# Weight sums on TensorE, a split soft-max in a new order, and a fourth pair of PSUM banks for one tile

## The chip, the cores and the metric

The kernel runs on one core of a Trainium2 chip. The metric is the device time of one execution in microseconds; the median of several runs is compared. Engines: PE is TensorE, DVE is VectorE, ACT is ScalarE, POOL is GpSimd, SP is SyncE (it only issues DMAs here).

## The reference

`x` is 8 images of 64 channels, 48 x 48 pixels, 32-bit. The reference normalises it by groups of two channels, makes from the result 8 logits a pixel (a 1x1 convolution) and a soft-max over them, makes 8 convolutions 3x3 (64 to 64 channels each), and adds, pixel by pixel, their weighted sum to `x`.

```python
def _gn(v, G=32, eps=1e-05): ...        # (v - mean) / sqrt(var + eps) over 2 channels x 48 x 48
...
logits = conv(x, coupler_w) + coupler_b[None, :, None, None]    # 8 sets
sel = softmax(logits, axis=1)
sel = sel / sel.sum(axis=1, keepdims=True)
conv = conv3x3(x, w).reshape(b_, s, oc, h_, w_) + bias[None, None, :, None, None]
return einsum('bschw,bshw->bchw', conv, sel)
...
x = x + _L0_conv_ref(_gn(x), ...)
```

## The kernel before, in words

**Work.** Two images at a time (a round; 4 rounds), their 128 channels on the 128 partitions. The 3x3 convolution uses a short form along the row: two neighbouring pixels are made of four products ("points") in place of six. For each point the input is a sum or difference of columns (`v_pts`) and the weights are sums of the three kernel columns: point 1 is w0 + w2 + w1, point 2 is w0 + w2 - w1 (both halved), the last two are w0 and w2. A round has 18 tiles (`TILES`) of 128 pixel pairs. Every factor is split in a 16-bit head and a 16-bit tail, so that a point is 4 or 5 matmuls of 512 columns (8 sets x 64 channels): three heads (one for each kernel row `r`) and one or two with tails (`point`). A tile has a pair of PSUM banks. PE writes points 1 and 2 into it (`first_points`); ACT copies bank 0 (`copy_m1`); DVE makes sum and difference (`seed`), which are the two pixels; PE adds points 3 and 4 (`last_points`); DVE multiplies by the selection (`multiply`, two passes), adds halves (`halve`), and POOL does the rest (`finish`).

**Banks.** Three pairs, `pair[i % 3]`, and two single banks: `side` with the logits and group sums, `w_bank` with the bound of the weights and warming matmuls.

**The start.** Each engine has a queue written out by hand, and the order of the calls at the end of its block is the order of execution. SP loads image pair 0 in three parts, two small matrices (for the group mean) and the weights `w_raw` in three rows, 768 KB each; then `first_fill(g, part)` copies input points from `v_head` and `v_tail` to the matmul operands `op` and `op_two`, five DMAs a call. ACT takes the largest absolute weight (`bound_of`), DVE and PE make of it one scale for all (`weight_bound`, L459 and L460, `scales`). DVE makes the sums of weights: `kernel_sum(r)` is w0 + w2 (L930), `kernel_point1(r)` adds w1 (L935), `kernel_point2()` subtracts it, all rows in one pass (L941). ACT rounds these to heads (`w_heads_of`, L607), DVE makes the tails (`first_point_tails` L917, `second_point_tails` L924, `last_point_tails` L948 and L951). The input has the same: heads on ACT (`first_heads`, L527), tails on DVE (`input_tails_of`, L977), for the first 24 image rows (part 0) and the rest (part 1). POOL makes the raw input points 1 to 3 (L1083), but its last two wait for the first weight head (`w_heads[0]`).

**Soft-max.** For the first round it is in two parts: the first 12 of 36 pixel columns before tile 0, the rest in pieces after tiles 0 to 3. `with_bias` is L713, `maximum` L720, `selection` L765 and L766. DVE's first pass of tile 0 (`multiply`, L791) waits for the first selection. After tile 4 `combine` makes the moments of the next image pair.

**PE's order at the start**: warming matmuls, group sums, warming matmuls of 32-bit ones (L450), the two bound matmuls, ten wide warming matmuls (L464), point 1 of tiles 0 and 1, the logits (54 small matmuls, L380), point 2 of tiles 0 and 1, both of tile 2, then the round: after the last points of tile i come the first points of tile i + 2. `load_ahead(1)` (ACT) loads the next image pair when all input points are made.

## Time and profile before

| | |
|---|---|
| median of 3 runs | 346.08 us (345.93 to 346.24) |
| profiled execution: time, span | 345.96 us, 344.2 us |
| mean granted clock of PE | 0.986 |
| PE busy | 325.8 us, 95% of the span |
| DVE busy | 282.4 us, 82% |
| POOL busy | 229.9 us, 67% |
| PE weight loads, beside the matmuls | 157.3 us, 46% |
| ACT busy | 108.9 us, 32% |

The span is from the first to the last instruction of the one execution that was profiled. A share is over the whole span and says nothing of a stage. A row of the timeline gives start and duration in us, engine, line, operation, output and inputs, shape and count; the next instruction of an engine may start before the one ahead has ended, so the cost of one is the distance of two starts.

### The profile page before, as it was taken

Reading aid. Unit: us, or ns where it says so; the run is one execution under the profiler, and the core shown is the slowest. Engines: PE = TensorE matmul, PEld = TensorE weight load, DVE = VectorE, ACT = ScalarE, POOL = GpSimd, SP = SyncE. Lnnn points to the kernel's source line nnn. Section 1 sums busy time; section 2 is a strip of 40 time slices with the busy share of each in tenths; the row PEclk is TensorE's granted clock in tenths of the full one; section 3 lists DMA queues with packets and bytes.
Section 4 is the critical chain, followed back from the end, with each engine's and each line's share of the span. In section 5 each row is a group of like instructions: output and inputs, shape, how many; then the busy total and the mean of one; then the engine's idle time right before and its main releaser. Section 6 shows DMA issues by size and latency. Waiting matters only on the chain.

```text
span 344.2 us, 5508 instructions
## 1 busy us (share of the span) xinstructions
PE 325.8 (95%) x1730; PEld 157.3 (46%) x1730; DVE 282.4 (82%) x508; ACT 108.9 (32%) x159; POOL 229.9 (67%) x329
## 2 busy tenths in 40 slices
PE   8959599999999899999999999999999899999993
PEld 8924244444544344444544344444544344444441
DVE  2789999997799697877799688887799687777786
ACT  1758262155411152164411152164411111111110
POOL 3420288899995489899874489899863499433343
PEclk9987999999999999999999999999999999999998
DMA  6543989507980298008980297009830496001002
GB/s 215 218 89 82 268 211 213 126 0 195 215 222 2 73 239 182 1 0 212 186 235 1 81 231 179 0 0 234 178 80 0 112 237 146 0 24 46 1 1 69
DMA packets 30230, 41.34 MB, mean 120 GB/s; under 512 B 2112, under 2 KB 23232, under 8 KB 29824
## 3 DMA queue, kind: packets, MB, share of 16 engines
q1 hardware_dynamic: 29328, 37.49, 45.9%
q10 hardware_dynamic: 880, 3.58, 3.4%
q8 instruction: 10, 0.16, 0.2%
q14 instruction: 12, 0.10, 0.1%
HBM read 11.97 MB, written 4.72 MB: 48 GB/s over the span
## 4 chain that ended last, share of the span: by engine, by line
PE 72%; DVE 23%; issue 4%; DVEq 1%; POOL 0%; POOLq 0%
PE pair L390 41%; PE pair L402 14%; PE pair L398 10%; PE w_bank L450 5%; DVE high L792 4%; DVE pair L791 3%; DVE half L800 3%; DVE pair L777 2%; DVE pair L775 2%; PE side L380 1%; DVE v_tail L977 1%; DVE w_tail L948 1%; DVE w_tail L917 1%; DVE w_tail L924 1%; DVE mix L759 0%
## 5 line engine op out<-in xcount | busy, mean ns | idle before, releaser
L390 PE MATMUL pair<-w_head,op 128*128 128x512 f16 x864 | 234.7, 381 | 9.0 <-DVE half L800 4.9
L390 PEld LDWEIGHTS pair<-w_head,op 128*128 128x128 f16 x864 | 83.4, 98 | 113.0 <-DVE half L800 9.5
L402 PE MATMUL pair<-w_tail,op 128*128 128x512 f16 x288 | 109.7, 381 | 0.5 <-DVE w_tail L951 0.5
L577 ACT ACTIVATE m_sb<-pair 128x512 f32<-128x512 f32 x72 | 42.9, 596 | 202.4 <-PE pair L402 194.0
L1106 POOL TENSOR_TENSOR quarter<-half 128x256 f32<-128x256 f32 x71 | 52.7, 742 | 64.6 <-DVE half L800 63.9
L791 DVE TENSOR_TENSOR pair<-pair,sel_now 128x512 f32<-128x512 f32 x71 | 49.4, 696 | 39.0 <-PE pair L402 38.9
L800 DVE TENSOR_TENSOR half<-pair,high 128x512 f32<-128x512 f32 x71 | 49.1, 692 | 9.5
L398 PE MATMUL pair<-w_tail,op_two 128*128 128x512 f16 x144 | 54.6, 379 | 0.1
L775 DVE TENSOR_TENSOR pair<-pair,m_sb 128x512 f32<-128x512 f32 x72 | 49.6, 689 | 0.0
L777 DVE TENSOR_TENSOR pair<-m_sb,pair 128x512 f32<-128x512 f32 x72 | 49.3, 684 | 0.0
L792 DVE TENSOR_TENSOR high<-pair,sel_now 128x512 f32<-128x512 f32 x71 | 48.3, 680 | 0.0
L402 PEld LDWEIGHTS pair<-w_tail,op 128*128 128x128 f16 x288 | 28.3, 98 | 34.9 <-DVE w_tail L951 0.8
L1110 POOL TENSOR_TENSOR mixed<-quarter 128x128 f32<-128x128 f32 x71 | 32.8, 462 | 5.6
L1116 POOL TENSOR_TENSOR y_out<-mixed,x_res 128x128 f32<-128x128 f32 x71 | 32.4, 457 | 5.7 <-POOL mixed L1110 0.3
L1069 POOL TENSOR_TENSOR v_tail<-v_pts,v_head 128x576 f16<-128x576 f32 x24 | 30.4, 1289 | 0.0
L398 PE MATMUL pair<-w_tail,op 128*128 128x512 f16 x72 | 27.8, 386 | 1.4 <-DVE w_tail L917 1.4
L1099 POOL TENSOR_TENSOR x_res<-x_res,bias_part 128x384 f32<-128x384 f32 x24 | 24.1, 1004 | 3.1 <-DMA x_res<-x_pix 0.6
L1078 POOL TENSOR_TENSOR v_pts<-x_raw 128x1152 f32<-128x1152 f32 (+1 forms) x12 | 24.9, 2078 | 0.0
L398 PEld LDWEIGHTS pair<-w_tail,op_two 128*128 128x128 f16 x144 | 14.1, 98 | 17.5 <-DVE w_tail L948 0.6
L1094 POOL TENSOR_TENSOR bias_part<-bias_all,sel_now 128x384 f32<-128x384 f32 x24 | 19.9, 829 | 0.1
L450 PE MATMUL w_bank<-ones 128*128 128x128 f32 x116 | 16.0, 308 | 1.6 <-POOL v_tail L1138 1.6
L450 PEld LDWEIGHTS w_bank<-ones 128*128 128x128 f32 x116 | 15.7, 223 | 1.6 <-POOL v_tail L1138 1.6
(107 smaller groups left out, 192.3 us busy)
## 6 DMA issues: line engine op xcount, KB each, us to landing
op<-v_head SPq DMA_DIRECT2D x14, 600.0 KB, 8.2
x_res<-x_pix SPq DMA_DIRECT2D x8, 576.0 KB, 6.5
op_two<-v_head SPq DMA_DIRECT2D x14, 300.0 KB, 9.2
op<-v_tail SPq DMA_DIRECT2D x14, 300.0 KB, 6.2
op<-v_head SPq DMA_DIRECT2D x14, 288.0 KB, 8.5
out<-y_out SPq DMA_DIRECT2D x7, 576.0 KB, 3.9
x_raw<-x ACTq DMA_DIRECT2D x3, 1152.0 KB, 9.7
w_raw<-weight SPq DMA_DIRECT2D x3, 768.0 KB, 8.5
```

What stands on the lines that cost most here:

```text
L390: nc.tensor.matmul(dst, op[b][:, 0, j, at + r * PW:at + r * PW + P], w_head[:, j, r, :], start=fresh and r == 0, stop=False, skip_group_ch ...
L398: nc.tensor.matmul(dst, op[b][:, 0, j, after] if j == 0 else op_two[b][:, j - 2, after], w_tail[:, j, 1, :], start=False, stop=False, skip ...
L402: return nc.tensor.matmul(dst, op[b][:, 1, j, at:at + P], w_tail[:, j, 0, :], start=False, stop=True, skip_group_check=True)
L450: nc.tensor.matmul(w_bank[:, 2 * P:3 * P], ones[:, :], ones[:, :], start=True, stop=True)
L577: act.activation(m1_sb[:, i % LOOK, :], pair[i % SETS_OF_BANKS][:, 0, :], ACT.Copy).then_inc(m1_copied, 1)
L775: dve.tensor_tensor(plus, minus, m1, ALU.add).then_inc(seeded, 1)
L777: dve.tensor_tensor(minus, m1, minus, ALU.subtract).then_inc(seeded, 1)
L791: dve.tensor_tensor(sets_of(i, 0), sets_of(i, 0), weights_of(i, 0), ALU.mult).then_inc(low_done, 1)
L792: dve.tensor_tensor(high[:, :, :, :], sets_of(i, SETS // 2), weights_of(i, SETS // 2), ALU.mult) \
L800: dve.tensor_tensor(half[:, i % LOOK, :, :, :].rearrange("p a s c -> p a (s c)"), pair[i % SETS_OF_BANKS][:, :, 0:N // 2], high[:, :, :, : ...
L1106: pool.tensor_tensor(quarter[:, :, :, :].rearrange("p a s c -> p a (s c)"), hf[:, :, 0:2, :].rearrange("p a s c -> p a (s c)"), hf[:, :, 2 ...
L1110: pool.tensor_tensor(mixed[:, :, :], quarter[:, :, 0, :], quarter[:, :, 1, :], ALU.add).then_inc(mixed_done, 1)
```

## The change

- `kernel_sum`, `kernel_point1` and `kernel_point2` of DVE go. PE makes point 1 of the weights: for each row three 32-bit matmuls of 512 columns with an identity matrix (a third matrix in `mats`) add w0, w2, w1 in PSUM, in banks of `pair[2]` and `pair[1]`. ACT and DVE read it there. DVE makes point 2 as point 1 - 2 w1, one pass a row.
- PE's 30 warming matmuls of 32-bit ones after the group sums go, and the ten wide ones become six. The bound matmuls come after seven of the nine new ones.
- The head of input point 0, part 0, is made by DVE (`first_head`). DVE's order changes: the input tails of all points of part 0 come before those of part 1 and before the tails of point 2 of the weights. ACT's order changes too; its edges come earlier.
- POOL's wait for `w_heads[0]` goes.
- Two of the five DMAs of the first fill are issued by ACT; the residual load `load_res(0, 0)` comes after the first fill and not after the third; `load_ahead(1)` comes after the heads of point 1 of the weights.
- `side` and `w_bank` become a fourth pair, `spare`, which tile 3 of the first round uses. PE makes point 1 of tiles 0, 1, 2, then point 2 of the same, the logits, then both of tile 3. In the first round tile i + 3 is begun after the last points of tile i, for i from 1 to 3. From tile 4 on the pair is `pair[(i + 2) % 3]`.
- The bias pass of the soft-max is one over all 36 pixel columns (the logits must leave `side` before tile 3 fills it); the pieces of the second part come partly one tile later, its last ones after tile 4.

```diff
-WARM_SMALL = (28, 30)
-WARM_WIDE = 10
+WARM_SMALL = 28
+WARM_WIDE = 6
-BIAS_FIRST_AT = (0, 0, 3, 4, 10, 13)
+BIAS_FIRST_AT = (0, 0, 4, 4, 10, 13)
...
-        side = ctx.enter_context(nc.psum_tensor("side", [P, N], F32))
-        w_bank = ctx.enter_context(nc.psum_tensor("w_bank", [P, N], F32))
+        spare = ctx.enter_context(nc.psum_tensor("spare", [P, 2, N], F32))
+        w_bank, side = (spare[:, a, :] for a in range(2))
+        w_pt1 = [pair[2][:, 0, :], pair[2][:, 1, :], pair[1][:, 1, :]]
...
+        def banks_of(i, begin=False):
+            if begin and i <= SETS_OF_BANKS:
+                return (pair + [spare])[i]
+            return pair[(i + SETS_OF_BANKS - 1) % SETS_OF_BANKS]
... SP
             first_fill(0, 0)
+            load_res(0, 0)
             first_fill(1, 0)
             first_fill(0, 1)
-            load_res(0, 0)
             first_fill(1, 1)
... PE, first_point
+                if not begin or i >= 2 * SETS_OF_BANKS + 1:
+                    pe.wait_ge(half_done, n * TILES + i + 1)
+                elif i > SETS_OF_BANKS:
+                    pe.wait_ge(half_done, i)
+                elif i == SETS_OF_BANKS and a == 1:
+                    pe.wait_ge(prep, 7)
... PE, start
-            warm_small(WARM_SMALL[1])
+            def kernel_point1(r, columns):
+                for kx in columns:
+                    last = nc.tensor.matmul(w_pt1[r], eye_mat[:, :], w_raw[:, r, kx, :], start=kx == 0, stop=kx == 1)
+                return last
+            pe.wait_ge(w_loaded[0], 16)
+            kernel_point1(0, (0, 2, 1)).then_inc(w_point1, 1)
+            pe.wait_ge(w_loaded[1], 16)
+            kernel_point1(1, (0, 2, 1)).then_inc(w_point1, 1)
+            pe.wait_ge(w_loaded[2], 16)
+            kernel_point1(2, (0,))
             (the two bound matmuls)
+            kernel_point1(2, (2, 1)).then_inc(w_point1, 1)
...
-            for i in range(2):
-                first_point(i, 0, 0, i == 0)
+            for i in range(3):
+                first_point(i, 0, 0, i == 0, True)
+            for i in range(3):
+                first_point(i, 1, 0, i == 0, True)
             (logits)
-            for i in range(2):
-                first_point(i, 1, 0, i == 0)
-            first_points(2, 0)
+            first_points(3, 0, True)
... ACT, the weight heads and the start
+                if k == 0 and rows.start < 2:
+                    act.wait_ge(w_point2, rows.stop)
...
+            def fill_beside():
+                pts, cols = slice(0, 2), slice(0, PW + FIRST_PAIRS)
+                act.wait_ge(h_first, 2)
+                act.dma_start(op[0][0:C, 1, pts, cols], v_head[0:C, pts, cols]).then_inc(first_in[0], 16)
+                act.dma_start(op_two[0][C:P, :, cols], ...).then_inc(first_in[0], 16)
             bound_of(2)
-            first_heads(0, 0)
+            fill_beside()
+            act.wait_ge(scale_ready, 1)
+            for k in range(2, NP):
+                edge(0, k)
+            first_heads(2, 0)
             act.wait_ge(w_chain, W_STEPS)
             (the three heads of point 1)
+            load_ahead(1)
+            first_heads(3, 0)
+            w_heads_of(1)
             first_heads(1, 1)
             first_heads(0, 1)
-            first_heads(2, 0)
-            w_heads_of(1)
-            first_heads(3, 0)
             w_heads_of(2)
             copy_m1(0, 0)
             w_heads_of(3)
... DVE, after the weight bound
-            kernel_sum(0) ... kernel_point1(2) ... kernel_point2()
+            def kernel_point2(r):
+                dve.wait_ge(w_point1, r + 1)
+                if r == 2:
+                    dve.wait_ge(w_heads[0], K)
+                dve.scalar_tensor_tensor(w_pt2[:, r, :], w_raw[:, r, 1, :], -2.0, w_pt1[r], ALU.mult, ALU.add) \
+                    .then_inc(w_point2, 1)
...
             first_input_point(0)
             input_tails_of(1, 0, 1)
+            first_head()
+            input_tails_of(0, 0, 2)
             first_input_point(1)
             weight_bound()
+            kernel_point2(0)
             scales()
+            kernel_point2(1)
+            first_point_tail(0)
+            first_point_tail(1)
+            kernel_point2(2)
+            first_point_tail(2)
+            input_tails_of(2, 0, 3)
+            input_tails_of(3, 0, 4)
+            second_point_tails()
             coupler_parts()
             input_tails_of(1, 1, 1)
             input_tails_of(0, 1, 2)
+            last_point_tails(2, 0)
+            last_point_tails(2, 1)
+            with_bias(0)
+            seed(0, 0, begin=True)
             maximum(0, 0)
             less_maximum(0, 0)
+            last_point_tails(3, 0)
             add_up(0, 0)
... POOL
-            pool.wait_ge(w_heads[0], 1)
```

The lines in brackets stand for lines that are unchanged.

## Rows read from the trace of the kernel before

**Rows 1.** Busy time by stages: stretch, its length, busy us (instructions) of each engine

```profile
core 0: us, PE busy (x) PEld busy (x) DVE busy (x) ACT busy (x) POOL busy (x), PEclk, DMA share, GB/s
10.00:20.00 10.00, 9.63 (x80) 8.73 (x80) 7.15 (x21) 6.89 (x10) 2.41 (x5) 1.00 0.44 155
20.00:30.00 10.00, 6.61 (x70) 2.97 (x69) 9.83 (x15) 6.73 (x10) 2.33 (x2) 0.70 0.23 49
...
150.00:250.00 100.00, 99.19 (x557) 46.40 (x556) 81.00 (x141) 38.41 (x53) 80.24 (x105) 1.00 0.57 133
```

**Rows 2.** Waits from 60 us to the end: total us, times, longest

```profile
PE pair L390 <- DVE half L800: 3.5, 4, 1.7
```

**Rows 3.** Timeline of DVE, the weights and the first input points

```profile
12.68 0.82 DVE L972 SCALAR_TENSOR_TENSOR v_pts<-x_raw,twice_mean 128x576 f32<-128x576 f32 x1
...
13.42 0.81 DVE L977 SCALAR_TENSOR_TENSOR v_tail<-v_pts,norm_scale,v_head 128x576 f16<-128x576 f32 x1
14.15 0.68 DVE L930 TENSOR_TENSOR w_sum<-w_raw 128x512 f32<-128x512 f32 x1
...
14.86 0.69 DVE L935 TENSOR_TENSOR w_pts<-w_sum,w_raw 128x512 f32<-128x512 f32 x1
...
15.47 0.82 DVE L972 SCALAR_TENSOR_TENSOR v_pts<-x_raw,twice_mean 128x576 f32<-128x576 f32 x1
...
17.53 0.14 DVE L984 TENSOR_REDUCE w_max<-w_max_part 64x1 f32<-64x3 f32 x1
...
18.43 0.16 DVE L989 TENSOR_SCALAR magnitude<-w_bank 128x2 int32<-128x2 int32 x1 [0.76 <-PE w_bank L460]
...
19.77 0.69 DVE L930 TENSOR_TENSOR w_sum<-w_raw 128x512 f32<-128x512 f32 x1
...
20.49 1.18 DVE L935 TENSOR_TENSOR w_pts<-w_sum,w_raw 128x512 f32<-128x512 f32 x1
21.60 0.77 DVE L959 TENSOR_SCALAR cw_pts<-cw_pair,half_scale 128x32 f16<-128x32 f32 x1
...
25.08 1.75 DVE L941 TENSOR_TENSOR w_pts<-w_sum,w_raw 128x1536 f32<-128x1536 f32 x1
```

**Rows 4.** Timeline of DVE, the soft-max and the first tiles

```profile
31.90 0.31 DVE L713 SCALAR_TENSOR_TENSOR logit<-side,undo,cb_all 128x96 f32<-128x96 f32 x1
...
41.05 0.70 DVE L791 TENSOR_TENSOR pair<-pair,sel_now 128x512 f32<-128x512 f32 x1
...
43.08 0.41 DVE L713 SCALAR_TENSOR_TENSOR logit<-side,undo,cb_all 128x192 f32<-128x192 f32 x1
...
61.37 0.69 DVE L775 TENSOR_TENSOR pair<-pair,m_sb 128x512 f32<-128x512 f32 x1
```

**Rows 5.** POOL's last input points in the timeline, and all passes of L700 (ns min/median/max)

```profile
19.97 2.37 POOL L1083 TENSOR_TENSOR v_pts<-x_raw 128x368 f32<-128x368 f32 x2 [7.59 <-ACT w_head L607]
...
L700 DVE SCALAR_TENSOR_TENSOR shift<-group,norm_scale x3: 271/274/1295, 71.7 to 225.7; 128x1 f32<-128x1 f32 x3
```

**Rows 6.** Timeline of PE: 32-bit warming matmuls, and two starts of a tile

```profile
10.85 6.94 PE L450 MATMUL w_bank<-ones 128*128 128x128 f32 x60
...
43.22 0.82 PE L390 MATMUL pair<-w_head,op 128*128 128x512 f16 x3 [1.46 <-DVE half L800]
...
47.33 0.81 PE L390 MATMUL pair<-w_head,op 128*128 128x512 f16 x3
```

**Rows 7.** Timeline, all engines: first weight heads, the fifth DMA, the first point

```profile
16.41 0.76 ACT L527 ACTIVATE v_head<-v_pts,norm_scale 128x576 f16<-128x576 f32 x1
...
19.17 1.33 ACT L607 ACTIVATE w_head<-w_pts,half_scale 128x512 f16<-128x512 f32 x2 [2.00 <-DVE scale L996]
...
20.01 0.59 SPq L308 DMA_DIRECT2D op<-v_tail  x1
...
23.02 0.82 PE L390 MATMUL pair<-w_head,op 128*128 128x512 f16 x3 [1.97 <-DMA op<-v_tail]
```

**Rows 8.** Two stretches of 1 us: PE's busy time, granted clock, DMA share, GB/s

```profile
24.00:25.00 1.00, 0.00 (x0) 0.52 0.00 0
...
30.00:31.00 1.00, 1.00 (x5) 0.56 0.08 20
```

More of the change, by code:

```diff
@@ L113, in program @@
         bias_all = sb("bias_all", [P, C])
[L114 to L115 removed]
+        mats = sb("mats", [P, 3, P])
+        mean_mat, diff_mat, eye_mat = (mats[:, k, :] for k in range(3))
         minus_half = sb("minus_half", [P, 1])
@@ L299, in first_fill @@
                 sp.dma_start(op[0][0:C, 0, pts, cols], heads[:, :, cols]).then_inc(landed, 16)
-                sp.dma_start(op[0][0:C, 1, pts, cols], heads[:, :, cols]).then_inc(fifth, 16)
+                if g or part:
+                    sp.dma_start(op[0][0:C, 1, pts, cols], heads[:, :, cols]).then_inc(fifth, 16)
                 sp.dma_start(op[0][C:P, 1, pts, below], heads[:, :, above]).then_inc(landed, 16)
-                if g == 0:
+                if g == 0 and part == 0:
+                    pass
+                elif g == 0:
                     sp.dma_start(op_two[0][C:P, :, cols], v_head[0:C, 1, cols].unsqueeze(1).to_broadcast([C, 2, width])) \
@@ L429, in last_points @@
                     pe.wait_ge(seeded, n * 2 * TILES + 2 * i + a + 1 + 2 * LOOK)
-                    point(b, 2 + a, t, pair[s][:, a, :], False, begin and i == 0).then_inc(y_done, 1)
+                    point(b, 2 + a, t, banks_of(i, begin)[:, a, :], False, begin and i == 0).then_inc(y_done, 1)
             def round_(n, more, begin=False):
@@ L522, in first_heads @@
                 act.wait_ge(v_first[k], ((1, 2), (2, 3), (2, 3), (2, 3))[k][part])
-                if k >= 2 and part == 0:
-                    edge(0, k)
+                if k >= 2:
                     act.wait_ge(edge_done, k - 1)
@@ L576, in copy_m1 @@
                 act.wait_ge(seeded, n * 2 * TILES + 2 * i + 2)
-                act.activation(m1_sb[:, i % LOOK, :], pair[i % SETS_OF_BANKS][:, 0, :], ACT.Copy).then_inc(m1_copied, 1)
+                act.activation(m1_sb[:, i % LOOK, :], banks_of(i, n == 0)[:, 0, :], ACT.Copy).then_inc(m1_copied, 1)
             def round_(n, more, ahead, copied=0):
@@ L766, in selection, with seed @@
                 dve.tensor_scalar(dst[0][:, px, :], mix[:, px, :], undo[:, 0:1], None, ALU.mult).then_inc(done, 1)
-            def seed(i, n, pixels=(0, 1)):
-                plus, minus = (pair[i % SETS_OF_BANKS][:, a, :] for a in range(2))
+            def seed(i, n, pixels=(0, 1), begin=False):
+                plus, minus = (banks_of(i, begin)[:, a, :] for a in range(2))
                 m1 = m1_sb[:, i % LOOK, :]
```

135 lines of the change are left out of this document (57 added, 78 removed).

## The prediction

> **What bounds the kernel now.** I read the busy time by stages first. From 20 to 30 us VectorE (DVE) is busy 9.83 us out of 10 and TensorE (PE) 6.61; from 150 to 250 us it is the other way round, PE 99.19 of 100 us against 81.00 for DVE [rows 1]. So the kernel has two stages: a start in which DVE is full, and a body in which PE is full. The list of waits after 60 us says where the second begins: PE still waited there for DVE's halving pass, 3.5 us in four places [rows 2]; the first of these is in the first round, soon after the seed of tile 6, and the others are at the turns of rounds and keep their distance from it. Whatever brings DVE's queue forward before that point brings the end forward by the same amount, if PE can follow; PE time saved later than that is another matter, and the change saves none.
>
> So I read the timeline of DVE from the first input point at 12.68 us to the first selection pass at 41.05 us and on to the seed of tile 6 at 61.37 us [rows 3, 4]. The queue stands still only once, for the matmul that spreads the weight bound: it ends the row at 17.53 + 0.14 = 17.67 and goes on at 18.43, 0.76 us. Everything else is work, and work that leaves this queue is a gain one for one.
>
> **What leaves DVE.** The six sums of kernel rows and the wide difference go. 14.15 to 15.47 is one sum and one first point, 1.32 us; the second pair costs the same and ends at 17.53; the third, 19.77 to 21.60, costs 1.83, and the difference at 25.08 costs 1.75 [rows 3]: 1.32 + 1.32 + 1.83 + 1.75 = 6.2 us. The coupler's first instruction has only 32 elements and took 0.77 us, because GpSimd was at work on its last two input points (19.97 to 22.34) [rows 3, 5]; these move to 12.4 us, since their wait for the first weight head is taken out, and the instruction falls to about 0.25: 0.5 us. The 0.76 us stall shrinks, because a new difference of weights now runs between the bound and the scales: I take 0.15 left, 0.6 us gained. The second bias pass of the soft-max, at 43.08, took 0.41 us [rows 4], and goes. Together 6.2 + 0.5 + 0.6 + 0.4 = 7.7 us.
>
> **What comes to DVE.** (a) Three differences from PSUM, 128x512 with one scalar. None such is in the trace; a pair of 512-wide passes takes 1.32 (0.66 each), and the scalar-tensor-tensor pass of 576 columns repeats after 0.73 [rows 3]. I take 0.66, as 512 wide: 1.98 us, between 1.8 and 2.2. (b) The head of the first input point, moved from ScalarE (ACT), 128x576: no such pass is in the trace; the two-input pass of the same width takes 0.82 [rows 3], half of it is the lower bound: I take 0.5. (c) The collision that the moved GpSimd work now has. At 20.49 the same 512-wide addition took 1.18 us instead of 0.69, with GpSimd's addition in flight, and the single-element pass of shift took 1.295 us against a median of 0.274 [rows 3, 5]: such a pass waits for the whole GpSimd instruction. From 12.4 us on two GpSimd instructions of some 0.75 us stand against the passes of 12.68 and 13.42, in turns: about 0.5 us before the first and 0.7 before the second, 1.2 us, between 0 and 1.9. (d) DVE's wait for ACT's first weight head, of which more below: 0.7, between 0 and 1.5. (e) The bias pass is now over all pixels in one: 0.31 for 96 columns and 0.41 for 192, so some 0.5 for 288, 0.16 more [rows 4]. (f) The end of the second soft-max part comes one tile later, side by side with the moments of the next image, while GpSimd adds two bias parts back to back; passes with two SBUF inputs will hit it more often: 0.4 us, between 0 and 1.5. Together 1.98 + 0.5 + 1.2 + 0.7 + 0.16 + 0.4 = 4.9 us. Net: 7.7 - 4.9 = 2.8 us.
>
> The rule behind (c) and (f) is in the Trainium skill, SBUF — State Buffer, section "Who interferes with whom": VectorE and GpSimd share a port pair, a VectorE instruction with two SBUF inputs contends with a GpSimd one that reads SBUF, and whichever is issued first holds it to its end. The trace agrees (1.18 against 0.69 us). The rule speaks against the part of the change that frees GpSimd's wait, and it also spares the new differences, whose one input is in PSUM. For (b), the Trainium skill, VectorE: DVE Perf Modes, "The perf-mode tier table", has a scalar pass of 32-bit SBUF data run at twice the rate of a two-tensor pass. No run here shows this for this shape; by it the sum would be 343.2, and at the single rate 343.6.
>
> **Does the rest follow?** PE's new sums: nine 32-bit matmuls of 512 columns against an identity. The trace has 30 of 128 columns (each is two records, 60) in 6.94 us at full clock, 0.231 each [rows 6]; four times that is 0.93 at most for one, 2.8 us a row. Begun at about 10.9 (the identity adds 64 KB ahead of the weights), rows 0 and 1 are done at 16.5 and the first third of row 2 at 17.4; the bound reaches PE at about 17.3, since DVE's queue ahead of it lost its sum pairs (2.65 us) and took on (b), (c) and one pass of 0.73 moved forward. So the bound matmuls start no later than now, and the scales are ready near 18.8. ACT: it is free of the bounds when it now starts its 16.41 activation. Then come two DMA issues, at 0.59 each as on SyncE [rows 7], two edges and one head of 0.77, and it reaches the first weight head at about 19.2, as now [rows 7]; each of the three takes 0.66. DVE has by then done two differences and waits from about 19.3 to 19.9: this is (d). The tails of the first kernel point are complete at about 22.9 against 25.08 now.
>
> PE's first points: six groups, five and four matmuls. The 19 matmuls of a tile take 47.33 - 43.22 = 4.11 us at full clock, 0.216 each [rows 6], so three groups of each kind are 27 x 0.216 = 5.8 us, the first two fifths of a group already done when the tails arrive at 22.9; they end at about 28.1. The logits wait for DVE's input tails at about 28.7 and take 1.5 us, and DVE comes to the bias pass at about 30.8. So PE has 0.5 us in hand, if its clock holds. Later, tile 3 has its own banks and its first points are done before the first halving ends; from there PE needs 4.11 us a tile, and DVE, from 41.05 to 61.37, did five tiles with all pieces of the soft-max between them in 20.3 us, 4.06 each [rows 4]. They are level for four tiles; followed pass by pass, PE has 0.1 to 0.5 us to spare. That the fourth pair of banks takes work from PE's path is therefore worth nothing by itself; it keeps PE level with the earlier DVE.
>
> **DMAs moved.** The residual load (576 KB), which now comes late, is issued ahead of the third and fourth fills, and the next image (1152 KB) near 21.4 instead of 33.24. Two of the first five fills are issued by ACT near 16.6 and 17.2. Today the fifth is issued at 20.01 and PE is released by it at 23.02, 3.0 us [rows 7]; then these land at 20.5 to 21.7, and they are needed at 21.3 to 22.2. The second group of fills is issued from 22.5 and needed only when tile 0 is seeded, near 31.8. Both are covered, the first with little to spare.
>
> **Forecast and rivals.** The profiled execution took 345.96 us with a span of 344.2, and the median is 346.08; the span falls by 2.8 to 341.4, and the time to 346.08 - 2.8 = 343.3.
>
> A, the ledger above, PE warm: 343.3. The bounds of (a) to (f) reach some 0.2, 0.3, 1.1, 0.7, 0 and 0.7 us to a side; independent of each other they make 1.4 (the root of their squares), so between 341.9 and 344.7. Chance 0.60.
>
> B, the clock. Today PE waits 1.97 us up to 23.02 and again until the tails are complete at 25.08 [rows 3, 7]; its granted clock falls to half at 24, 1.2 GHz, and comes back at 30 to 31 [rows 8]. In the new order PE is busy with the last sums to 19.7 and with six wide warming matmuls to 21.0, and then waits only some 0.3 and 0.8 us. That speaks for a clock that holds. If a landing is late it falls again, and 5.8 us of first points take some 9: 3.4 us late, less the 0.9 in hand, 2.5 us on the path. Time 345.7, for half the fall 344.6. Chance 0.17. It is the case that would hide the gain.
>
> C, PE is the slower partner in the stretch of tiles 2 to 5, where it has 0.1 to 0.5 us to spare, or its clock falls in the holes before it (some 1.9 us idle between 33.9 and 36.2): DVE waits about 1.2 us. Time 344.5. Chance 0.13.
>
> D, slower than before: the seven 32-bit matmuls that stand in PE's queue in front of the bound matmuls. The first landing of the weights is at about 10.8. At 0.93 us they are done at 17.4, just when the bound comes. Everything waits for the scales behind them: three weight heads, all tails. If one takes 1.85 us, as at half clock, they are done at 23.8, 6.5 us late, and the time is 343.3 + 6.5 = 349.8; at 1.4 us each, 3.2 us late, they already use up the whole gain (346.5). From 1.35 us each on the change loses. Against it: the clock is at full level, 2.4 GHz, from 10 to 20 us with 32-bit matmuls [rows 1, 6]. Chance 0.06.
>
> E, no change: DVE's gain is given back where PE is full, if fills land late at the first use of the second half of image 0's operands: 346.1. Against it: GpSimd makes the tails that they carry as soon as the first selection is there, and so these move with DVE. Chance 0.04.
>
> Differences of 0.2% (0.7 us) are about what a measurement of this kernel can tell. Faster by more: A, C, and B but for its worst quarter: 0.60 + 0.13 + 0.13 = 0.86; within: E and the rest of B, 0.08; slower: D, 0.06. The range from 342.0 to 345.6 holds A and C and most of B.
>
> **What would show it.** DVE's first selection pass near 38.3 instead of 41.05, the seed of tile 6 near 58.6 instead of 61.37; the passes of 12.68 and 13.42 longer or later beside GpSimd; one DVE wait for a weight head near 19.5; bound matmuls at 17.4; the granted clock 1.00 between 24 and 30. Wrong would be: a first selection pass that starts earlier without an earlier end (C or E), or scales later than 19 us (D).

## The result, and the profile after

The changed kernel takes 343.36 us (median of 4 runs, 342.96 to 343.65), the kernel before 346.16 us beside it (345.93 to 346.37): a ratio of 0.9918, 95% interval 0.9901 to 0.9936. It is 2.8 us faster. The forecast was 343.3. The executions of the changed kernel do not scatter evenly: with the four of here and the five of experiment 11, five took 342.96 to 343.07 us and four 343.65 to 343.66, and the median of 343.36 lies in the gap between the two groups. Experiment 7 shows where they part.

| | before | after |
|---|---|---|
| profiled execution: time, span | 345.96, 344.2 us | 343.07, 341.3 us |
| mean granted clock of PE in it | 0.986 | 0.999 |
| first selection pass of DVE | 41.05 us | 37.53 us |
| seed of tile 6 | 61.37 us | 58.41 us |
| DVE busy | 282.4 us | 279.9 us |

The windows of the changed kernel stand against [rows 1, 8] (columns as there):

```profile
20.00:30.00 10.00, 8.85 (x88) 4.34 (x87) 9.80 (x17) 9.49 (x12) 0.00 (x0) 1.00 1.03 291
24.00:25.00 1.00, 1.00 (x7) 0.43 (x5) 0.97 (x2) 1.00 (x3) 0.00 (x0) 1.00 1.09 371
30.00:31.00 1.00, 1.00 (x8) 0.32 (x5) 0.97 (x3) 0.29 (x1) 0.00 (x0) 1.00 1.10 217
150.00:250.00 100.00, 99.19 (x558) 46.41 (x557) 81.41 (x143) 36.71 (x52) 80.34 (x106) 1.00 0.59 136
```

The two stages are as they were: DVE full at the start, PE full in the body, and in the body PE's 99.19 us of 100 are the same. Nothing was gained there. Between 20 and 30 us PE now has 8.85 us of work instead of 6.61, at full clock; DMA has grown from 49 to 291 GB/s there, because residual and next image are loaded now; the first point waited 0.55 us for its tails (21.78 below), and went on long before DVE needed it.

The timeline of DVE in the changed kernel, from the first input point on, stands against [rows 3, 4]:

```profile
12.95 1.09 DVE L1006 SCALAR_TENSOR_TENSOR v_pts<-x_raw,twice_mean 128x576 f32<-128x576 f32 x1
13.96 1.35 DVE L1018 SCALAR_TENSOR_TENSOR v_tail<-v_pts,norm_scale,v_head 128x576 f16<-128x576 f32 x1
15.24 0.51 DVE L1012 TENSOR_SCALAR v_head<-v_pts,norm_scale 128x576 f16<-128x576 f32 x1
15.78 0.82 DVE L1018 SCALAR_TENSOR_TENSOR v_tail<-v_pts,norm_scale,v_head 128x576 f16<-128x576 f32 x1
...
17.25 0.14 DVE L1025 TENSOR_REDUCE w_max<-w_max_part 64x1 f32<-64x3 f32 x1
17.32 0.67 DVE L974 SCALAR_TENSOR_TENSOR w_pt<-w_raw,pair 128x512 f32<-128x512 f32 x1
18.15 0.16 DVE L1030 TENSOR_SCALAR magnitude<-spare 128x2 int32<-128x2 int32 x1 [0.17 <-PE spare L488]
...
18.76 0.68 DVE L974 SCALAR_TENSOR_TENSOR w_pt<-w_raw,pair 128x512 f32<-128x512 f32 x1
19.61 1.53 DVE L959 SCALAR_TENSOR_TENSOR w_tail<-pair,half_scale,w_head 64x512 f16<-64x512 f32 x2 [0.17 <-ACT w_head L637]
21.17 0.69 DVE L974 SCALAR_TENSOR_TENSOR w_pt<-w_raw,pair 128x512 f32<-128x512 f32 x1
21.78 0.74 DVE L959 SCALAR_TENSOR_TENSOR w_tail<-pair,half_scale,w_head 128x512 f16<-128x512 f32 x1
...
30.39 0.52 DVE L752 SCALAR_TENSOR_TENSOR logit<-spare,undo,cb_all 128x288 f32<-128x288 f32 x1
...
37.53 0.70 DVE L833 TENSOR_TENSOR pair<-pair,sel_now 128x512 f32<-128x512 f32 x1
...
43.03 0.70 DVE L767 TENSOR_TENSOR logit<-logit,top 128x192 f32<-128x192 f32 x1
...
54.85 0.77 DVE L801 TENSOR_TENSOR mix<-logit,top 128x192 f32<-128x192 f32 x1
...
56.52 0.84 DVE L714 TENSOR_TENSOR offset<-mean_var,center 128x1 f32<-128x1 f32 x1
...
57.53 0.96 DVE L717 SCALAR_TENSOR_TENSOR mean_var<-offset,minus_offset,mean_square 128x1 f32<-128x1 f32 x1
58.41 0.69 DVE L817 TENSOR_TENSOR pair<-pair,m_sb 128x512 f32<-128x512 f32 x1
```

The reader is to see three things. The sums are gone, and the queue stops for less than 0.2 us where it stood for 0.76 (18.15) and where a wait for the weight head was feared (19.61). The first selection pass comes 3.52 us earlier. Up to the seed of tile 6 only 2.96 of them are left: the passes with two SBUF inputs at 43.03, 54.85, 56.52 and 57.53 are up to twice as long as the same passes elsewhere, or more.

PE of the changed kernel, the timeline:

```profile
11.05 6.28 PE L476 MATMUL pair<-w_raw,mats 128*128 128x512 f32 x14 [0.27 <-DMA w_raw<-weight]
17.54 0.35 PE L487 MATMUL spare<-tiny,ones 128*128 128x2 f32 x2 [0.21 <-DVE w_max L1025]
...
17.97 1.96 PE L476 MATMUL pair<-w_raw,mats 128*128 128x512 f32 x4
19.77 1.46 PE L493 MATMUL spare<-v_head 128*128 128x512 f16 x6
21.78 0.82 PE L399 MATMUL pair<-w_head,op 128*128 128x512 f16 x3 [0.55 <-DMA op<-v_tail]
...
58.64 0.35 PE L376 MATMUL spare<-mean_var,mats 128*128 128x2 f32 x2 [1.86 <-DVE mean_var L717]
...
61.77 0.82 PE L399 MATMUL pair<-w_head,op 128*128 128x512 f16 x3 [0.28 <-DVE half L842]
```

Seven 32-bit matmuls of 512 columns (14 records) stand in front of the bound matmuls; the last two (four records) take 19.77 - 17.97 = 1.80 us, 0.90 each. The matmuls of the last row are the first of PE's four waits for the halving from 60 us on; the total is the same 3.5 us as in [rows 2]:

```profile
PE pair L399 <- DVE half L842: 3.5, 4, 1.7
```

### The profile page after: what moved, and what is told of

The parts are those of the page before. It is cut to its first block, busy times and chain, and to the rows that moved or that the text cites. A ratio compares the mean times of both kernels' runs of the same rounds, so it can differ in the third digit from the quotient of the medians.

```text
span 341.3 us, 5410 instructions
## 1 busy us (share of the span) xinstructions
PE 324.0 (95%) x1684; PEld 152.7 (45%) x1684; DVE 279.9 (82%) x504; ACT 108.1 (32%) x158; POOL 229.7 (67%) x329
## 4 chain that ended last, share of the span: by engine, by line
PE 67%; DVE 23%; issue 4%; POOL 2%; DMA 2%; DVEq 1%; ACT 0%
PE pair L399 42%; PE pair L411 14%; PE pair L407 10%; DVE high L834 4%; DVE pair L833 3%; DVE pair L817 3%; DVE half L842 2%; DVE pair L819 2%; DMA x_raw<-x 2%; POOL v_pts L1123 2%; DVE v_tail L1018 1%; PE spare L389 1%; DVE w_tail L982 1%; DVE mix L801 1%; DVE w_tail L966 1%
## 5 line engine op out<-in xcount | busy, mean ns | idle before, releaser
L399 PE MATMUL pair<-w_head,op 128*128 128x512 f16 x852 | 230.3, 379 | 7.0 <-DVE half L842 5.3
L399 PEld LDWEIGHTS pair<-w_head,op 128*128 128x128 f16 x852 | 82.0, 98 | 109.1 <-DVE half L842 7.9
L411 PE MATMUL pair<-w_tail,op 128*128 128x512 f16 x284 | 107.6, 379 | 0.5 <-DVE w_tail L985 0.5
L842 DVE TENSOR_TENSOR half<-pair,high 128x512 f32<-128x512 f32 x70 | 48.4, 692 | 10.1 <-DVE high L834 1.0
L407 PE MATMUL pair<-w_tail,op_two 128*128 128x512 f16 x142 | 53.8, 379 | 0.0
L817 DVE TENSOR_TENSOR pair<-pair,m_sb 128x512 f32<-128x512 f32 x71 | 48.9, 689 | 0.0
L819 DVE TENSOR_TENSOR pair<-m_sb,pair 128x512 f32<-128x512 f32 x71 | 48.6, 684 | 0.0
L834 DVE TENSOR_TENSOR high<-pair,sel_now 128x512 f32<-128x512 f32 x70 | 47.6, 680 | 0.0
L407 PE MATMUL pair<-w_tail,op 128*128 128x512 f16 x71 | 26.9, 379 | 0.0
L1202 POOL TENSOR_TENSOR v_pts<-v_pts,norm_scale 128x576 f32<-128x576 f32 x2 | 2.3, 1148 | 23.0 <-DVE sel_now L808 22.9
L545 ACT ACTIVATE v_head<-v_pts 128x1152 f16<-128x1152 f32 x12 | 14.0, 1163 | 0.4
```

What stands on the lines that cost most here:

```text
L399: nc.tensor.matmul(dst, op[b][:, 0, j, at + r * PW:at + r * PW + P], w_head[:, j, r, :], start=fresh and r == 0, stop=False, skip_group_ch ...
L407: nc.tensor.matmul(dst, op[b][:, 0, j, after] if j == 0 else op_two[b][:, j - 2, after], w_tail[:, j, 1, :], start=False, stop=False, skip ...
L411: return nc.tensor.matmul(dst, op[b][:, 1, j, at:at + P], w_tail[:, j, 0, :], start=False, stop=True, skip_group_check=True)
L817: dve.tensor_tensor(plus, minus, m1, ALU.add).then_inc(seeded, 1)
L819: dve.tensor_tensor(minus, m1, minus, ALU.subtract).then_inc(seeded, 1)
L834: dve.tensor_tensor(high[:, :, :, :], sets_of(i, SETS // 2, begin), weights_of(i, SETS // 2), ALU.mult) \
```

## The experiments

There are twelve experiments: ten kernels, then the changed kernel and kernel 9 once more. Each was timed beside the kernel before.

**1. The kernel before with its clock kept up.** Nine more wide warming matmuls of before.

```diff
-WARM_WIDE = 10
+WARM_WIDE = 19
```

> The kernel before with 19 wide warming matmuls in place of 10 (nine more, 1.9 us at full clock, filling TensorE's hole from 21.1 to 23.0 us). Queue theory: the end moves with VectorE's queue, and TensorE had some 2 us in hand there (logits done at 29.9 us, bias pass at 31.9), so about 346.1 us whether the clock falls or not. Clock theory: the changed kernel's gain is the clock that no longer falls at 24 us; then this kernel takes 343.5 to 344.5 us.

346.35 us (12 runs) against 346.31, ratio 0.9993 (0.9978 to 1.0008). The window of this kernel in which the kernel before had 0.52 [rows 8]:

```profile
24.00:25.00 1.00, 0.00 (x0) 0.00 (x0) 0.97 (x3) 0.72 (x1) 0.00 (x0) 1.00 0.00 0
```

The clock stayed at 1.00, and the time did not move: the restored clock between 24 and 30 us is not where the 2.8 us come from. The first selection pass of DVE starts at 40.89 us here and at 41.05 in the kernel before, and the bound of the weights is 0.14 us earlier too. So the fallen clock costs the kernel before nothing: DVE is the one everybody waits for.

**2. The changed kernel without the fourth pair.** Three pairs of banks throughout and the old order of tiles.

```diff
-            if begin and i <= SETS_OF_BANKS:
-                return (pair + [spare])[i]
-            return pair[(i + SETS_OF_BANKS - 1) % SETS_OF_BANKS]
+            return pair[i % SETS_OF_BANKS]
...
-                    if begin and 0 < i <= SETS_OF_BANKS:
-                        first_points(i + SETS_OF_BANKS, n, True)
...
-            first_points(3, 0, True)
```

> The changed kernel without the fourth pair of banks: tile i in pair i mod 3, first points of tile i + 2 after the last points of tile i, tile 3 begun after the first halving. Queue theory: the last points of each tile come at the same time, TensorE's 1.94 us for tile 3 fills the hole of 1.86 us at 56.8 to 58.6 us: 343.4 us, within 0.5. Bank theory: the work taken off TensorE's path is the gain or part of it: 344.4 to 345.4 us.

343.4 us (6 runs) against 346.31, ratio 0.9906 (0.9883 to 0.9929): the same as with the fourth pair. PE now stands idle for 3.4 us, from the end of the logits at 29.6 us to the last points of tile 0. Its clock is at full level up to 30 us and falls in the microsecond after, early in this idle time; PE's timeline, and windows of this kernel:

```profile
32.98 1.46 PE L397 MATMUL pair<-w_head,op 128*128 128x512 f16 x3 [3.40 <-DMA op<-v_tail]
```

```profile
30.00:31.00 1.00, 0.00 (x0) 0.00 (x0) 1.00 (x3) 0.00 (x0) 0.00 (x0) 0.65 1.07 234
...
33.00:36.00 3.00, 3.00 (x8) 1.08 (x9) 2.90 (x8) 0.56 (x2) 0.00 (x0) 0.50 0.52 117
```

What DVE feels of both is one wait, and its first selection pass starts no later than with the fourth pair (37.53):

```profile
37.47 0.70 DVE L823 TENSOR_TENSOR pair<-pair,sel_now 128x512 f32<-128x512 f32 x1 [0.44 <-PE pair L409]
```

The fourth pair moves PE's idle time to another place (from 29.5 to 33 us without it, to the 1.86 us before 58.64 with it) and its worth in time is not to be told from nothing: the two intervals reach 0.8 us to a side. The six runs (343.29 to 343.5) lie between the two groups of the changed kernel, which this kernel does not have.

**3. The changed kernel with its sums on VectorE.** Point 1 of the weights is again made by six DVE additions, into SBUF; order, banks, soft-max and moved DMAs stay as changed, and 27 small warming matmuls stand where the sums were.

```diff
-            kernel_point1(0, (0, 2, 1)).then_inc(w_point1, 1)
...
+            warm_small(27)
...
+            kernel_sum(0)
+            kernel_sum_point1(0)
...
+            kernel_sum(2)
+            kernel_sum_point1(2)
```

> The changed kernel with the weight sums back on VectorE (three pairs of a sum and a first point, each some 1.32 us, written to SBUF) and 27 small warming matmuls on TensorE in place of the nine 32-bit ones; order, clock and banks as in the changed kernel. Queue theory: 3 x 1.32 = 3.96 us more in VectorE's queue, some 0.2 of it in its waits: about 347.1 us. Rival, the gain is from order, clock or banks: 343.4 to 344.5 us.

348.45 us (8 runs) against 346.31, ratio 1.0053 (1.0034 to 1.0072): 5.1 us more than the changed kernel and 2.1 more than the kernel before, where 347.1 was expected. The timeline of its DVE:

```profile
16.43 0.68 DVE L969 TENSOR_TENSOR w_sum<-w_raw 128x512 f32<-128x512 f32 x1
...
17.76 0.81 DVE L1013 SCALAR_TENSOR_TENSOR v_pts<-x_raw,twice_mean 128x576 f32<-128x576 f32 x1
...
34.76 0.52 DVE L749 SCALAR_TENSOR_TENSOR logit<-spare,undo,cb_all 128x288 f32<-128x288 f32 x1 [0.64 <-PE spare L392]
...
41.89 0.70 DVE L830 TENSOR_TENSOR pair<-pair,sel_now 128x512 f32<-128x512 f32 x1
```

The pairs cost 1.33 (16.43 to 17.76), 1.44 and 1.33, together 4.1 us, and 0.64 is a wait for PE's logits. That makes 4.7; the first selection pass is 4.36 us later than in the changed kernel, among other things because the wait for the first weight head (0.17) is gone and the stage begins 0.08 earlier. PE goes from the first points to the logits without a pause, and a part of these first points ran at half clock; a window of this kernel:

```profile
27.00:29.00 2.00, 2.00 (x6) 0.76 (x5) 1.97 (x4) 2.00 (x4) 0.00 (x0) 0.50 0.93 306
```

This is the mechanism of case B, with 0.64 us of price. The seed of tile 6 is 4.36 us later as well (62.77), and the profiled execution as a whole 4.97. The 0.6 us between arise right behind that seed: after 1.85 us of idle PE before the group sums the clock falls once more, to 0.50 from 65 to 67 us. Experiment 7 shows the same with its rows.

**4. The changed kernel without wide warming.**

```diff
-WARM_WIDE = 6
+WARM_WIDE = 0
```

> The changed kernel without its six wide warming matmuls: TensorE then waits from 19.8 to 21.8 us. If the granted clock falls at 24 us as in the kernel before, case B of the prediction is seen and priced: the first points last about 9 us in place of 5.8, 345.0 to 345.7 us. If it holds, 343.4 us.

343.51 us (342.84 to 344.37, 6 runs) against 346.31, ratio 0.9907 (0.9881 to 0.9932): no change. PE is idle for 1.7 us here, after the 32-bit sums, and the clock holds:

```profile
20.00:22.00 2.00, 0.28 (x2) 0.20 (x3) 1.94 (x4) 1.57 (x4) 0.00 (x0) 1.00 0.87 209
```

Its runs fall into groups like those of the changed kernel: two with a mean clock of 0.995 and 1.0 took 342.84 and 342.94 us, three with 0.990 and 0.991 took 343.5 to 343.62, and one with 0.987 took 344.37. The profiled execution is one of the three. Its clock falls not at 24 us but near 60 (0.55 from 59 to 62 us), as in experiment 7. Whether the six matmuls make a run like that of 344.37 rarer, six runs can't tell.

**5. The kernel before with the sums on TensorE alone.** Its order, banks and soft-max unchanged; all nine sums stand around the bound matmuls as in the change.

```diff
+            kernel_point1(0, (0, 2, 1)).then_inc(w_point1, 1)
...
-            kernel_sum(0)
-            kernel_point1(0)
...
-            kernel_point1(2)
...
-                dve.tensor_tensor(w_pts[:, 1, :, :], w_sum[:, :, :], w_raw[:, :, 1, :], ALU.subtract).then_inc(w_point2, 1)
+                for r in range(K):
+                    dve.scalar_tensor_tensor(w_pts[:, 1, r, :], w_raw[:, r, 1, :], -2.0, w_pt1[r], ALU.mult, ALU.add) \
+                        .then_inc(w_point2, 1)
```

> The kernel before with the weight sums alone moved: the three sums and three first points leave VectorE (1.32 + 1.33 + 1.83 us), TensorE makes them with the identity as in the changed kernel, the wide difference (1.75 us) becomes three differences from PSUM (about 2.0 us). Order, banks, soft-max and DMAs as before. Queue theory: the first two pairs were partly in front of the weight bound, which is ready only at 16.5 us, so VectorE gains there no more than the 0.4 us by which the scales come earlier; the third pair counts in full, 1.83, less 0.25: about 2.0 us, 344.2 us. Rival, the sums are worth their whole 4.5 us less 0.25: 342.0 us. Rival, the order is what gains: 346.2 us.

344.42 us (11 runs) against 346.21, ratio 0.9953 (0.9938 to 0.9968), 0.2 from the expectation of the queue theory; the first selection pass is at 39.37 us, 1.68 earlier than before. The timeline of its DVE at the weight bound:

```profile
16.74 0.15 DVE L1001 TENSOR_REDUCE w_max<-w_max_part 64x1 f32<-64x3 f32 x1 [1.57 <-ACT w_pts L629]
17.86 0.16 DVE L1006 TENSOR_SCALAR magnitude<-w_bank 128x2 int32<-128x2 int32 x1 [0.97 <-PE w_bank L472]
```

In the old order the freed time turns in part into waiting: DVE stands 1.57 us for ACT's bound and 0.97 for PE. The four kernels make a table of medians, each measured beside the kernel before:

| | all else as before | all else as changed |
|---|---|---|
| sums on VectorE | 346.2 | 348.45 |
| sums on TensorE | 344.4 | 343.4 |

The sums alone give 1.8 us; all the rest of the change takes 2.1 without them and gives 1.0 with them. So they belong together. One reason is in the rows: the new order moves input tails and the first head in front of the weight bound. With the sums gone from there that fills the freed time (the magnitude pass is at 18.15 us, before at 18.43); with a sum still there it delays the bound (19.39 in experiment 3). The first selection pass of experiment 3 is 0.84 us later than before; the other 1.3 us of its loss arise behind it, 0.56 in the longer passes up to the seed of tile 6, the rest mostly in the clock that falls after it. "All else" is order, banks, the single bias pass and the moved DMAs together; only the banks (experiment 2), the wide warming matmuls (4) and GpSimd's wait (6) were tried by themselves.

**6. The changed kernel with POOL's wait back.** It tests the collision that the prediction priced at 1.2 us.

```diff
+            pool.wait_ge(w_heads[0], 1)
```

> The changed kernel with GpSimd's wait for the first weight head put back, so that its last two input points run near 19.6 to 21.2 us and not beside VectorE's passes of 12.95 and 13.96. If the collision is on the path, as the ledger counts it (0.82 us measured in the changed kernel's trace), 342.6 us. If it is hidden, because the weight bound then waits for ScalarE's third bound (16.8 us) and for seven 32-bit matmuls (17.4 us) anyway, 343.2 to 343.5 us; the next image's load is then issued about 1 us later and does not matter.

343.36 us (5 runs) against 346.21, ratio 0.991 (0.9894 to 0.9925): the same median. The timeline of its DVE:

```profile
12.84 0.82 DVE L1006 SCALAR_TENSOR_TENSOR v_pts<-x_raw,twice_mean 128x576 f32<-128x576 f32 x1
13.58 0.81 DVE L1018 SCALAR_TENSOR_TENSOR v_tail<-v_pts,norm_scale,v_head 128x576 f16<-128x576 f32 x1
...
16.70 0.15 DVE L1025 TENSOR_REDUCE w_max<-w_max_part 64x1 f32<-64x3 f32 x1 [0.29 <-ACT w_junk L644]
```

The passes are short again (0.82 and 0.81 instead of 1.09 and 1.35), so the collision is real; but DVE now waits 0.29 us for ACT's bound, the magnitude pass comes 0.54 us earlier (17.61), and the first selection pass only 0.36 (37.17). So more than half of the collision lies in time that DVE loses in another way without it. The median does not show the remaining 0.36, because it falls into another of the two groups: the two runs with a mean clock of 0.999 and 1.0 took 342.74 and 342.77 us, against 342.96 to 343.07 of the changed kernel, and the three with 0.985 to 0.992 took 343.36 to 343.6, against 343.65. Like with like, POOL's wait gives some 0.2 us, on five runs.

**7. The changed kernel with the bound late.** Twelve more 32-bit matmuls of 128 columns, some 2.8 us, in front of the bound matmuls.

```diff
+            warm_small(12)
```

> The changed kernel with twelve 32-bit matmuls of 128 columns (12 x 0.231 = 2.8 us) in TensorE's queue in front of the two bound matmuls. Case D of the prediction: no slack there, so the scales and all behind come 2.7 us later: 346.1 us. If there is slack: 343.4 to 344.5 us.

345.95 us (12 runs) against 346.21, ratio 0.9979 (0.9968 to 0.999): 2.6 us more than the changed kernel. The magnitude pass is 2.18 us later (20.33), the first selection pass too (39.71), the seed of tile 6 2.19 (60.60). There is no slack in front of the bound matmuls. Case D's mechanism is right; only its size did not occur.

The twelve runs again make two groups: four with a mean clock of 0.999 or 1.0 took 345.16 to 345.19 us, eight with 0.992 took 345.89 to 346.16. The first four are 2.2 us above the corresponding group of the changed kernel (342.96 to 343.07), which is what was put in; the 2.6 of the medians holds a different share of the two groups. The profiled execution is one of the eight, and shows where the clock is lost: PE's timeline, and a window of this kernel:

```profile
60.82 0.35 PE L376 MATMUL spare<-mean_var,mats 128*128 128x2 f32 x2 [1.85 <-DVE mean_var L718]
```

```profile
62.00:66.00 4.00, 4.00 (x12) 1.51 (x11) 3.87 (x7) 0.00 (x0) 2.87 (x6) 0.57 0.54 126
```

PE has stood for 1.85 us before the group sums, the same wait as that of 1.86 before 58.64 in the changed kernel, and 1.6 us after it is back at work its clock falls to half for some 3.4 us. The wait for the halving at the turn of the round ends at 115.04, 2.85 us later than in the changed kernel, where the seed of tile 6 was 2.19 later: the fall costs 0.66 us. Both traced executions of the changed kernel (0.999) have the same wait and a clock of 1.00 after it. The traces of experiments 3 and 4 show the wait and the fall. So the step of 0.65 us between the two groups of the changed kernel is most likely this fall. It is not shown directly: no execution of its group at 343.65 was traced, and one of its four runs at 343.65 has a mean clock of 0.999, which this does not explain.

**8. The changed kernel with the next image's moments after tile 6.** The hole of 1.86 us in PE's queue before 58.64 is a wait for DVE's one-element passes. Moved two tiles later, they no longer stand ahead of the seed of tile 6; scaled points, heads and tails of the next image move by a tile or more.

```diff
-                    if more and i == 4:
+                    if more and i == 4 and not begin:
...
+                        if begin and i == 6:
+                            combine(n + 1)
...
+                    tails_at = (9, 10, 11, 12) if begin else TAILS_TILE
```

> The changed kernel with the moments of the next image pair moved in the first round only: VectorE combines them after the seed of tile 8 in place of before that of tile 6, and group sums, variance, scale, heads and tails follow one or two tiles later. Refined queue theory: from tile 6 on VectorE has time to spare (3.24 us of passes against TensorE's 4.11 a tile), so the 2.25 us that the moments took at 56.2 to 58.4 us leave the path and TensorE's hole of 1.86 us closes: about 341.5 us. Rival, the wait only moves to tile 8 to 10 or to the end of the round: 343.0 to 343.4 us.

346.8 us (11 runs) against 346.21, ratio 1.001 (0.9998 to 1.0022): the expectation fell. The hole is gone and the seed of tile 6 stands at 56.11, 2.3 us earlier; but the input tails of the next image, which POOL makes, are late for the logits. PE's timeline, and a window of this kernel:

```profile
87.15 0.21 PE L389 MATMUL spare<-cw_pts,v_head 128*128 128x32 f16 x2 [4.56 <-POOL v_tail L1112]
```

```profile
85.00:90.00 5.00, 2.85 (x58) 2.03 (x59) 0.00 (x0) 0.00 (x0) 4.84 (x7) 0.53 0.68 146
```

PE waits 4.56 us, its mean granted clock from 85 to 90 us is 0.53, and DVE does nothing for these 5 us. One wait was removed and a longer one took its place.

**9. The same, and the logits a tile later.** VectorE's bias pass and maximum and GpSimd's fifth bias part follow.

```diff
-                    if more and i == 11:
+                    if more and i == (12 if begin else 11):
...
-                    if more and i == 12:
+                    if more and i == (13 if begin else 12):
```

> The kernel with the later moments, and now what waits for them is later too: TensorE makes the next round's logits after the first points of tile 14 and not of tile 13, VectorE's bias pass and maximum follow one tile later, and GpSimd adds its fifth bias part after the second input tails and not before. Theory: the 4.6 us that TensorE stood before the logits in the kernel with later moments were this alone (the second input tails came at 87.1 us, TensorE was there at 82.6), and with it gone the 2.2 us gained at tile 8 last: 341.5 us. Rival, the queues of the round's end are full too and the time comes back there: 343.0 us or more.

342.12 us (341.94 to 343.8, 5 runs) against 346.18, ratio 0.9871 (0.9839 to 0.9903): 0.6 short of the expectation, 341.5.

**10. The logits two tiles later**, the soft-max after them pressed together.

> As the kernel with the logits one tile later, but two tiles later, with the soft-max of the next round pressed together after tiles 14 to 16. If the tails are still not there at the earlier place this one is the faster of the two, 341.5 us; if they are, the soft-max stands closer to the turn of the round, where VectorE is waited for, and it is slower than the other by up to 1 us.

343.29 us (6 runs) against 346.18, ratio 0.9918 (0.989 to 0.9946): the gain is given back at the turn of the round, where PE waits 2.23 us for the halving in one place.

**11 and 12. The changed kernel and kernel 9 side by side**, since their intervals almost touched.

> The changed kernel itself, on the same chip as the next run, so that the two are compared directly. Both theories expect 343.4 here, ratio to the kernel before 0.992.

> The kernel of after_late_logits12b again, beside the changed kernel on one chip. Theory one (TensorE's hole at 56.8 us, where it waits for the moments, is on the path, and closing it is worth about 1 us): 342.2, at least 0.7 under the changed kernel beside it. Theory two (the 1.2 us seen were scatter between runs): within 0.4 us of the changed kernel, 343.2.

The changed kernel: 343.0 us (342.98 to 343.66, 5 runs), ratio 0.9914 (0.9901 to 0.9927). Kernel 9: 342.84 us (341.99 to 343.77, 6 runs), ratio 0.9906 (0.9886 to 0.9926). Side by side the medians are 0.16 us apart and not to be told apart. That is the number of theory two (within 0.4 us), not that of theory one; but theory two's reason, scatter, does not fit, since the runs again fall into two groups. The two profiled executions of kernel 9 say why. The first row is of experiment 9, the second of this one, both PE's timeline:

```profile
111.22 1.31 PE L399 MATMUL pair<-w_head,op 128*128 128x512 f16 x3 [2.02 <-DVE half L843]
```

```profile
111.22 0.82 PE L399 MATMUL pair<-w_head,op 128*128 128x512 f16 x3 [2.02 <-DVE half L843]
```

Up to this instruction the two are level, and both have waited 2.02 us for the halving. Then the clock of one falls (1.31 us for three matmuls), that of the other stays at full (0.82). The window from 110 to 115 of the first and of the second:

```profile
110.00:115.00 5.00, 3.78 (x10) 1.43 (x11) 2.55 (x5) 0.60 (x1) 3.41 (x5) 0.66 0.17 51
```

```profile
110.00:115.00 5.00, 3.78 (x18) 1.78 (x19) 2.55 (x5) 0.60 (x1) 3.42 (x5) 1.00 0.16 50
```

Their spans are 342.0 and 340.3 us. Over all 11 runs of kernel 9, the seven with a mean clock of 0.997 or more took 341.94 to 342.15 us and the four with 0.992 to 0.993 took 343.54 to 343.8. The nine runs of the changed kernel took 342.96 to 343.07 us or 343.65 to 343.66. So closing the hole before 58.64 is worth some 0.9 us (343.0 less 342.1) where the clock holds in both kernels, and nothing where it falls in both (343.54 to 343.8 against 343.65). With that hole the fall near 60 us is gone, at 0.65 us; but PE's wait at the turn of the round has grown from 1.69 to 2.02 us, and there the clock now falls in four of eleven runs, at 1.6 us. That is read from traces and the clocks of the runs, and wasn't tried by itself. Kernel 9 is no shown improvement on the changed kernel; the median of its 11 runs is 342.14, that of the nine 343.07.

## Why the prediction was right, by its own steps

**The mechanism.** What DVE's queue gains before the first selection pass comes out at the end. Experiment 7 shows it by the reverse sign (2.18 us in, 2.2 out where the clock holds in both kernels), the changed kernel by its own: the seed of tile 6 comes 2.96 us earlier, PE's long wait for the halving at the turn of the first round ends at 112.19 instead of 115.10 us, 2.91 earlier, the span is 2.9 shorter and the median 2.8. That the median meets the forecast to 0.1 us is luck in part: it lies between a group at 343.0 (3.1 us faster than before) and one at 343.65 (2.5).

**What leaves DVE**: forecast 7.7 us. Sums and difference are gone, the coupler's first instruction has fallen from 0.77 to 0.24, the queue stands 0.17 for the bound (forecast 0.15). By the distance of starts that is 7.3 us ahead of the first selection pass, as forecast (7.7 less the 0.4 of the second bias pass).

**What comes**: forecast 4.9 us, 4.5 of them ahead of the first selection pass; there 3.6 were measured.
- (a) The differences repeat after 0.61 (21.17 to 21.78) and 0.68 (18.76 to 19.61, less the 0.17 wait), against 0.66: right.
- (b) The first head costs 15.78 - 15.24 = 0.54, forecast 0.5. The row of 0.51 us stands beside 0.82 for the two-input pass of the same 576 columns. The Trainium skill, VectorE: DVE Perf Modes, "The perf-mode tier table", has the scalar pass at twice the rate; the trace agrees but for a fixed part, since 0.51 is more than half of 0.82 (how large a fixed part, no run here shows).
- (c) The collision with POOL costs (13.96 - 12.95 - 0.74) + (15.24 - 13.96 - 0.73) = 0.27 + 0.55 = 0.82 us, forecast 1.2: mis-sized. Experiment 6 shows that without it the first selection pass would come only 0.36 earlier.
- (d) The wait for the first weight head is 0.17, forecast 0.7: mis-sized, the largest miss ahead of the first selection pass. The prediction put ACT's two DMA issues, 1.2 us, ahead of its next work; in ACT's timeline they run largely beside an activation that is under way (ACTq is ACT's queue of DMA issues):

```profile
15.20 1.49 ACT L644 ACTIVATE w_junk<-w_raw 64x1536 f32<-64x1536 f32 x1
15.78 0.71 ACTq L658 DMA_DIRECT2D op<-v_head  x1
16.52 0.63 ACTq L659 DMA_DIRECT2D op_two<-v_head  x1
...
17.20 0.68 ACT L518 ACTIVATE v_pts<-x_raw,group 128x48 f32<-128x48 f32 x2 [0.42 <-issue]
...
18.89 1.91 ACT L637 ACTIVATE w_head<-pair,half_scale 128x512 f16<-128x512 f32 x3 [0.38 <-DVE scale L1037]
```

Only 0.42 us of them are left as a gap (17.20), and ACT then waits 0.38 for the scales: it was ready before them.
- (e) The bias pass takes 0.52 us, its first part took 0.31 before; by the distance of starts 0.44 against 0.34, 0.10 more, forecast 0.16. The second part is gone, as forecast.
- (f) Mis-sized the other way. From the first selection pass to the seed of tile 6 it is 58.41 - 37.53 = 20.88 us, before 20.32 [rows 4], though 0.4 of a bias pass has left the stretch: 1.0 us against a forecast of 0.4. It lies in the two-input passes beside POOL: 0.70, 0.77, 0.84 and 0.96 in the rows above. By the distance of starts these four cost 0.36, 0.42, 0.29 and 0.60 us more than the same passes before. In return a pass of the kernel before that had run beside POOL has its short time again, 0.31 us; its row in DVE's timeline of the kernel before:

```profile
56.07 0.81 DVE L766 TENSOR_SCALAR sel_now<-mix,undo 128x192 f32<-128x192 f32 x1
```

The pass of L717 takes 0.35 as its median (three of them, 0.346 to 0.959 us). The rule was named in the prediction: the Trainium skill, SBUF — State Buffer, "Who interferes with whom". The rows agree with it; what was wrong was the count of hits.

The start of the stage is 0.27 later than before (12.95 against 12.68), which no step had. So the first selection pass came 3.5 us earlier where 2.75 was forecast, and 0.56 of that was given back by the seed of tile 6. The right total rests in part on (c) and (d), 0.4 and 0.5 us too dear, against (f), 0.6 too cheap, and the late start. The range had a slip too: the root of the squares of the stated bounds is 1.5, not 1.4.

**The rivals.** B: the clock did not fall between 24 and 30; experiment 1 shows that its fall in the kernel before cost nothing, experiment 3 that in the new order a fall before the logits can cost 0.64 us. Both are under the 2.5 that the prediction gave it. A fall that no rival had at its place is that near 60 us after the hole before 58.64 (0.65 us, experiment 7). C did not occur: the timeline of DVE shows no wait for PE between 37.53 and 58.41, and in experiment 2, where PE ran at half clock before that stretch, the one wait ahead of it is 0.44 us. D: the seven matmuls ended before the bound came (PE waited 0.21 us for it), at 0.90 us each; 0.93 was forecast, and experiment 7 confirms that they have nothing to spare. E: nothing was lost in the body. The fourth pair "worth nothing by itself" agrees with experiment 2, within its interval.

## What to carry to other kernels

When one engine's queue is the bound at the start, count what leaves and what comes to it, pass by pass, up to the last point at which somebody still waits for it: the distance of that one row from before to after is the gain. Work taken off a queue pays fully only if the next item is ready; here the sums alone gave 1.8 us and the rest of the change alone cost 2.1, together they gave 2.8. Before a hole is closed, look whose wait comes next: the same move cost 3.4 us with the logits in place and gave some 0.9 with them one tile later, and even that hangs on the clock after the following hole. And look at the single runs and their clocks before two medians are compared: in experiments 6, 7 and 12 the median moved with the share of runs in which the clock fell.

## What was not expected of the hardware

- Two DMA issues in ACT's queue (0.71 and 0.63 us, from 15.78 to 17.15) ran beside the activation that was under way; after it a gap of 0.42 us was left.
- A 32-bit matmul of 512 columns takes 0.90 us at full clock, against 0.216 for a 16-bit one [rows 6].
- The clock held through 1.7 us of idle PE between 20 and 22 us without warming matmuls (experiment 4), fell early in a wait of 3.4 us (experiment 2, between 30 and 31 us, where PE had stopped at 29.6), and after the same wait it fell in one execution and held in another: after 2.02 us in experiments 9 and 12, after 1.85 us in experiment 7 and 1.86 in the changed kernel. In experiments 7 and 9 PE was back at work when it fell.
- A pass of a single element a partition with two SBUF inputs took 0.96 us instead of 0.35 with POOL at work. A pass with one tensor input was hit as well: 0.81 us instead of 0.31 (56.07 in the kernel before).
